# One quantising chain a step, base products copied straight into the residual's rows, and two reorderings in a GPS layer kernel

## The chip, the cores and the metric

The kernel runs on one core of a Trainium2 chip. The metric is the device time of one execution in microseconds, lower is better. TensorE is called PE here, VectorE DVE, ScalarE ACT, GpSimd POOL and SyncE SP. Before the change three runs took 913.72, 914.22 and 915.47 us, median 914.22 us.

## The reference

There are 1250 nodes with 1024 features and 40,000 directed edges sorted by target. Cut to what matters:

```python
xn  = layernorm(x)                                            # 1250 x 1024
# graph attention, 4 heads of 64, each node also an edge to itself
h   = (xn * rsqrt(mean(xn**2) + 1e-6) * rms_w) @ W_down       # 1250 x 256
e   = einsum(leaky_relu((h@Wl)[src] + (h@Wr)[dst]), att)
gnn = segment_sum(softmax_by_dst(e) * (h@Wl)[src], dst) @ W_up
# linear attention without softmax: 16 heads of 64
mix = (per head (q @ k.T) * 1/8 @ v) @ Wo.T + bo              # q, k, v = xn @ W.T + b
x2  = x + gnn + mix
# feed-forward part in fake fp4: blocks of 16 values, an fp8 scale for each
g, u   = nvfp4_linear(ln(x2), gate_w), nvfp4_linear(ln(x2), up_w)   # 1250 x 512
out    = x2 + nvfp4_linear(silu(g) * u, down_w)
```

`nvfp4_linear` takes the largest absolute value of each block of 16, makes an fp8 scale from it, divides, rounds to the fp4 values (0, 0.5, 1, 1.5, 2, 3, 4, 6 with sign), multiplies by the scale again, and multiplies the matrices.

## The kernel before, in words

The nodes lie in 10 chunks (0 to 9) of 128 rows, one row a partition. The program of each engine is written out by hand; semaphores alone tie the engines together, so each engine does its instructions in the order of the code.

**Start.** SP loads x chunk by chunk. DVE takes each chunk's mean and variance (L1271 to L1274), POOL the root (L573), and `norm(c)` (L1266) normalises it; in the code `norm(c-1)` stands behind chunk c's statistics. PE turns the normalised chunk (L772), ACT copies it to `xhat_t` (L1075), and the first product groups (L749) multiply it by W_down, which ACT has scaled (L1080). `one_hots(q)` (L1305) on DVE makes marks with which PE counts receivers (L757).

**Products and rounds.** Since the linear attention has no softmax, its matrices are folded together: 16 groups each of `gram`, `p`, `kv`, `t1`, `t2`, then 2 short `bias` groups and 14 `base` groups, which are x-hat times the folded matrix for chunks 0 to 6 (EARLY = 7), two halves of 512 columns each. A group is 8 fp32 products with 512 columns (16 records in the trace) into one PSUM bank; group n uses the bank of group n-4 and waits until DVE or ACT has taken that. ACT takes the base groups into the memory of `xhat_t`, DVE the bias groups. Beside this DVE, ACT and POOL run the graph attention in 62 rounds (number 61 is the last). A planner (`round_of`, from L982) walks over the groups with costs (PRODUCTS_AT, GROUP_STEP) and sets in which round each taking stands.

**Between.** When the rounds end, `send_attention` (L660) scatters the last chunk of the attention to HBM by an indirect DMA, SP loads the whole attention back (L523, tile `acc_sb`), and PE turns it (L918). Meanwhile the residual's rows `base` (part of tile `big_b`) are put together by DMA: SP writes the bias row into chunks 0 to 8 (L520), POOL adds x by 10 accumulating DMAs (`add_x`, L682) and then adds the base products by 7 more (`lay_base`, L688, 128x8x128 elements from `xhat_t`).

**Feed-forward steps.** `x2(c, h)` on PE (L908) makes a half chunk of the attention's product; for c >= 7 it first makes 8 fp32 products of the linear part (L905). `residual` on DVE (L1603) adds it to `base`. X2_PLAN says in which step each of them stands. Steps k = -1 to 12 then do, each engine in its own order:

- DVE: `tail_scales(k)` (hidden product L1569, block maxima L1258 on 512 and on 1024 columns, nine small operations L1223 to L1233 on up to 96 columns), `rows_rounded(k+1)` (eight operations L1247 to L1255 on 1024 columns, gives q), residuals of (k, 1), `hidden_rounded(k-1)` (the same eight on 512 columns, gives h), residuals of (k, 2).
- PE: turn q of chunk k+1 (L927), the x2 halves of (k, 0), turn h (L949) and multiply down (L960) for chunk k-2, gate and up products for chunk k+1 (L938).
- ACT: copy the turned q (L1164), normalise chunk k+2 (L1023, L1024), copy the turned h (L1191), silu of chunk k+1 (L1199), scale the down product (L1156); `deviation` (L1141 to L1146) takes the variance of a chunk as soon as its residuals are in.
- POOL: the root (L714) behind each deviation, and the DMA that adds the scaled product to the stored x2 (L720). The last chunk is finished on DVE (L1608).

## Time and profile before

| | before |
|---|---|
| median of three runs | 914.22 us (913.72 to 915.47) |
| the profiled execution's own time | 911.83 us |
| its span | 910.0 us |
| granted TensorE clock, mean | 0.972 of full speed |
| PE busy | 857.1 us (94%) |
| DVE busy | 818.1 us (90%) |
| ACT busy | 550.7 us (61%) |
| POOL busy | 500.0 us (55%) |
| bytes moved by DMA | 118.37 MB, mean 130 GB/s |

The span is the time from the first to the last recorded instruction; what lies around it is 911.83 - 910.0 = 1.83 us. Busy shares are means over stages with different limits: of the page's 40 slices of 22.75 us, PE shows 7 tenths in the 32nd (705 to 728 us), where DVE, in the slices 31 to 33, shows 6, 0 and 6; in the feed-forward slices behind it DVE shows 9 until the last, PE 5 to 9.

### The profile page before, as it was taken

The numbers are of one execution on the slowest core, as the hardware profiler recorded it, in microseconds if no ns is written. First come the engines' busy times: TensorE is split into PE (matmuls) and PEld (weight loads), VectorE is DVE, ScalarE is ACT, GpSimd is POOL, SyncE is SP. The second block draws the span as 40 slices with busy tenths as digits, with TensorE's granted clock in tenths as the row PEclk, the third lists the DMA queues.
The fourth block names the chain that finished last, engine by engine and source line by source line (L and its number), as shares of the span: only waits on it lengthen the run. The fifth ranks groups of instructions, "written<-read, shape, count | busy, mean of one in ns | idle before, by whom it ended". The sixth has DMA issues, their size and how long they took to land.

```text
span 910.0 us, 9566 instructions
## 1 busy us (share of the span) xinstructions
PE 857.1 (94%) x2744; PEld 419.5 (46%) x2754; DVE 818.1 (90%) x987; ACT 550.7 (61%) x1949; POOL 500.0 (55%) x529
## 2 busy tenths in 40 slices
PE   5999999999999999999999999998999797999755
PEld 5895455644444444444444444443444343444322
DVE  6999996789999999999999999999996069999996
ACT  3313123356677877779898988888998053343342
POOL 3400658577666767877777787877774400010011
PEclk7999999999999999999999999999999899999878
DMA  9322525463655433663336633339939970122224
GB/s 299 109 95 54 173 92 181 142 199 90 81 170 180 103 88 90 193 218 94 101 100 192 193 97 100 101 91 237 356 97 196 191 133 24 63 53 56 39 46 88
DMA packets 73443, 118.37 MB, mean 130 GB/s; under 512 B 29399, under 2 KB 43380, under 8 KB 73370
## 3 DMA queue, kind: packets, MB, share of 16 engines
q0 software_dynamic: 28560, 64.21, 30.5%
q1 hardware_dynamic: 44826, 53.52, 18.3%
q8 instruction: 22, 0.36, 0.2%
q14 instruction: 35, 0.29, 0.1%
HBM read 89.15 MB, written 17.17 MB: 117 GB/s over the span
## 4 chain that ended last, share of the span: by engine, by line
DVE 50%; PE 32%; POOL 7%; issue 6%; DMA 3%; ACT 1%; SPq 0%; ACTq 0%; DVEq 0%; POOLq 0%
PE acc L749 22%; DVE acc_sb L1498 9%; DVE z L1650 9%; DVE turned L1490 8%; DVE turned L1648 8%; POOL round_mem L551 6%; PE turned L905 2%; PE acc L908 1%; DVE round_mem L1258 1%; DVE round_mem L1247 1%; PE acc L938 1%; PE turned L960 1%; DVE big_a L1458 1%; DVE z L1655 1%; DVE round_mem L1248 1%
## 5 line engine op out<-in xcount | busy, mean ns | idle before, releaser
L551 POOL DMA_INDIRECT round_mem<-msg_table,idx x352 | 347.9, 988 | 99.8 <-issue 80.6
L1133 ACT ACTIVATE round_mem<-round_mem,pz 128x65 f32<-128x65 f32 x1408 | 353.9, 398 | 6.4 <-DVE acc_sb L1498 2.5
L749 PE MATMUL acc<-wslot,big_a 128*128 128x512 f32 x512 | 220.3, 592 | 0.0
L749 PEld LDWEIGHTS acc<-wslot,big_a 128*128 128x128 f32 x512 | 97.1, 190 | 121.5 <-issue 121.3
L1498 DVE TENSOR_REDUCE acc_sb<-round_mem 128x260 f32<-128x1820 f32 (+1 forms) x62 | 121.6, 1961 | 7.6 <-ACT round_mem L1133 5.1
L1123 ACT ACTIVATE pz<-z 128x7 f32<-128x7 f32 (+1 forms) x248 | 55.4, 296 | 93.7 <-DVE z L1655 93.4
L749 PE MATMUL acc<-wslot,big_b 128*128 128x512 f32 x256 | 110.0, 592 | 0.0
L749 PE MATMUL acc<-big_b,wslot 128*128 128x512 f32 x256 | 110.0, 592 | 0.0
L1490 DVE TENSOR_TENSOR turned<-round_mem,turned 128x1560 f32<-128x1560 f32 (+1 forms) x62 | 105.4, 1701 | 3.7 <-DMA round_mem<-msg_table,idx 1.6
L1650 DVE TENSOR_REDUCE z<-turned 128x24 f32<-128x1560 f32 (+1 forms) x62 | 105.1, 1695 | 2.1
L1648 DVE SCALAR_TENSOR_TENSOR turned<-turned,att_sb 128x1536 f32<-128x1536 f32 (+1 forms) x62 | 103.5, 1670 | 0.0
L749 PE MATMUL acc<-big_a,xhat_t 128*128 128x512 f32 x224 | 96.6, 593 | 2.7 <-ACT big_a L1070 2.7
L749 PE MATMUL acc<-big_b 128*128 128x512 f32 (+3 forms) x240 | 80.4, 494 | 0.0
L749 PEld LDWEIGHTS acc<-big_b,wslot 128*128 128x128 f32 x256 | 48.6, 190 | 61.2 <-issue 61.0
L749 PEld LDWEIGHTS acc<-wslot,big_b 128*128 128x128 f32 x256 | 48.6, 190 | 61.2 <-issue 61.2
L749 PEld LDWEIGHTS acc<-big_a,xhat_t 128*128 128x128 f32 x224 | 42.4, 190 | 56.9 <-issue 52.4
L714 POOL TENSOR_TENSOR rstd<-small,minus_half 128x1 f32<-128x1 f32 x10 | 6.4, 639 | 98.7 <-ACT small L1146 98.7
L749 PEld LDWEIGHTS acc<-big_b 128*128 128x128 f32 x240 | 42.8, 193 | 35.2 <-issue 29.5
L669 POOL TENSOR_TENSOR round_mem<-acc_sb,pz 128x260 f32<-128x260 f32 x62 | 45.9, 740 | 21.0 <-DVE acc_sb L1498 20.2
L720 POOL DMA_DIRECT2D out_x<-acc_sb x9 | 7.9, 878 | 71.2 <-ACT acc_sb L1156 71.2
L1060 ACT COPY big_a<-acc 128x512 f32<-128x512 f32 x16 | 9.2, 586 | 57.8 <-PE acc L749 42.3
L1199 ACT ACTIVATE round_mem<-acc,cscale 128x512 f32<-128x512 f32 x10 | 6.9, 688 | 59.3 <-PE acc L938 59.3
(233 smaller groups left out, 1031.6 us busy)
## 6 DMA issues: line engine op xcount, KB each, us to landing
round_mem<-msg_table,idx POOLq DMA_INDIRECT x352, 2.8
big_b<-in_x SPq DMA_DIRECT2D x9, 512.0 KB, 8.8
big_b<-big_b SPq DMA_DIRECT2D x9, 512.0 KB, 14.0
big_b<-in_x POOLq DMA_DIRECT2D x9, 512.0 KB, 12.4
out_x<-big_b SPq DMA_DIRECT2D x9, 512.0 KB, 3.6
out_x<-acc_sb POOLq DMA_DIRECT2D x9, 512.0 KB, 5.4
wslot<-in_wv_t SPq DMA_DIRECT2D x2, 2048.0 KB, 10.5
wslot<-in_wk_t SPq DMA_DIRECT2D x2, 2048.0 KB, 9.6
```

Of the source, the lines that this page charges most:

```text
L551: pool.indirect_dma_start(xg[g % 4][:, j, :], None, msg_table, bass.IndirectOffsetOnAxis(idx[:, c, j0 + j:j0 + j + 1], 0)).then_inc(xg_in[ ...
L669: nc.gpsimd.tensor_tensor(halves_of[g % 3][:, :, :, n].rearrange("p i (h d) -> p i h d", d=MR), running[c].rearrange("p (i h d) -> p i h d ...
L749: mm = nc.tensor.matmul(o(acc[:, n % 4, :]), a, b, start=first, stop=last)
L905: nc.tensor.matmul(to, xhat_t[:, k, c * NC:(c + 1) * NC], mat_a[:, k, h * HALF:(h + 1) * HALF], start=(k == 0), stop=False)
L908: mm = nc.tensor.matmul(to, gnn_tr[:, k, c * NC:(c + 1) * NC], wup_sb[:, k, h * HALF:(h + 1) * HALF], start=(c < EARLY and k == 0), stop=( ...
L1060: nc.scalar.copy(mat_a[:, m, h * HALF:(h + 1) * HALF], a).then_inc(t, 1)
L1123: ins = nc.scalar.activation(pz[:, g % 2, 0:slots + 1, h], z[:, g % 3, 0:slots + 1, h], ACT.Exp, scale=-1.0, bias=z[:, (g + 1) % 3, top_sl ...
L1133: ins = nc.scalar.activation(to[:, :, j], xg[g % 4][:, j, h * HR + 1:(h + 1) * HR], ACT.Copy, scale=pz[:, g % 2, j, h:h + 1])
L1490: return nc.vector.tensor_tensor(m4[:, 0:n], xg[g % 4][:, 0:n, :].rearrange("p j (h d) -> p j h d", d=HR)[:, :, :, 0:MR], receiver.unsquee ...
L1498: nc.vector.tensor_reduce(running[c].rearrange("p (i f) -> p i f", i=2), halves_of[g % 3][:, :, :, 0:n + 1], AX.X, ALU.add).then_inc(sum_d ...
L1648: step(nc.vector.scalar_tensor_tensor(m4[:, 0:slots, :, 1:MR], m4[:, 0:slots, :, 1:MR], 0.0, att_sb[0:NC].unsqueeze(1).to_broadcast([NC, s ...
L1650: step(nc.vector.tensor_reduce(zz[:, 0:slots, :], m4[:, 0:slots], AX.X, ALU.add))
```

## The change

It does five things.

1. **One chain a step.** The normalised rows and silu/hidden of a step now lie side by side in one slab of 1536 columns. The block maximum is one instruction, the first seven quantising operations run once on 1536 columns, and the eighth is split: q (1024), then h (512). `step_rounded` stands right behind `tail_scales`, ahead of the residual of (k, 1).
2. **Base products in place.** ACT copies the base groups straight into `base`. The bias row is no longer written first but added: SP loads x plainly for chunks 7 and 8 only, POOL adds x for chunks 0 to 6 and 9 (`add_x`) and the bias row for chunks 0 to 8 (`add_bias`). The 7 DMAs of `lay_base` are gone; of these 512 KB DMAs 19 are left of 26. Six stand ahead of the last scatter, three x behind the attention's load, ten in steps -1 and 1.
3. **Order of the base groups.** Both first halves of chunks 0 and 1 come ahead of the bias groups; the second halves, which need the last `t2` takings, behind them.
4. **Gated rows turned right behind q.** `turn_hidden(k-2)` stands right behind `turn_q(k+1)` ahead of the x2 products; ACT normalises chunk k+2 before it copies the turned q, and silu waits for h_done instead of hid_done.
5. **Start.** `norm(1)` stands ahead of chunk 2's statistics.

```diff
-PRODUCTS_AT, GROUP_STEP = 169, {"p0c": 2.0, "bias": 1.0}
+PRODUCTS_AT, GROUP_STEP = 166, {"p0c": 2.0, "bias": 1.0}
...
-BIAS_SUMS_AT, X_AT = 40, 61
+BIAS_SUMS_AT, AHEAD = 40, 3
+BETWEEN = {-2: {"x": (0, 1, 2), "bias": ()}, -1: {"x": (), "bias": (0, 1)}, 0: {"x": (), "bias": (2,)}}
...
-         "base": [(c, h) for c in range(EARLY) for h in range(2)]}
+         "base": [(c, h) for h in range(2) for c in range(2)] + [(c, h) for c in range(2, EARLY) for h in range(2)]}
...
-    g += [("bias", 0, "dve"), ("bias", 1, "dve")] + [("base", i, "act") for i in range(2 * EARLY)]
+    g += [("base", i, "act") for i in range(2)] + [("bias", i, "dve") for i in range(2)]
+    g += [("base", i, "act") for i in range(2, 2 * EARLY)]
...
+        NB = (D + I) // QB
+        slab = [tail_mem[0:NC, i * (D + I):(i + 1) * (D + I)] for i in range(2)]
+        ln2, silu = [a[:, 0:D] for a in slab], [a[:, D:D + I] for a in slab]
+        row_cells, row_steps = (tail_mem[0:NC, 6 * I + 768 * i:6 * I + 768 * (i + 1)].bitcast(BF16) for i in range(2))
...
-            sp.wait_ge(acc_taken["dve"], taken[index_of["bias", 1]])
-            for c in range(C - 1):
-                sp.dma_start(base[:, c, :], bias_bc).then_inc(x_in[c], 16)
+            sp.wait_ge(acc_full, index_of["bias", 1] + 1)
+            for c in range(EARLY, C - 1):
+                sp.dma_start(base[:, c, :], x[c * NC:(c + 1) * NC, :]).then_inc(x_in[c], 16)
...
             def add_x(c):
                 n = rows(c)
-                if c < C - 1:
-                    pool.wait_ge(x_in[c], 32)
+                if c < EARLY:
+                    pool.wait_ge(acc_taken["act"], taken[index_of["base", ORDER["base"].index((c, 1))]])
                 else:
                     for i in range(C - 1):
-                        pool.wait_ge(x_in[i], 32)
-                pool.dma_start(base[0:n, c, :], x[c * NC:c * NC + n, :], accum_op=ALU.add).then_inc(x_added[c], 16)
-
-            def lay_base(c):
-
-                pool.wait_ge(acc_taken["act"], taken[index_of["base", ORDER["base"].index((c, 1))]])
-                pool.wait_ge(x_added[c], 16)
-                pool.dma_start(base[:, c, :].rearrange("p (k n) -> p k n", k=KB), base_at[c], accum_op=ALU.add).then_inc(base_added[c], 16)
+                        pool.wait_ge(bias_added[i], 16)
+                pool.dma_start(base[0:n, c, :], x[c * NC:c * NC + n, :], accum_op=ALU.add).then_inc(x_added[min(c, EARLY)], 16)
+
+            def add_bias(c):
+
+                if c < EARLY:
+                    pool.wait_ge(x_added[c], 16)
+                else:
+                    pool.wait_ge(x_in[c], 32)
+                pool.wait_ge(acc_taken["dve"], taken[index_of["bias", 1]])
+                pool.dma_start(base[:, c, :], bias_bc, accum_op=ALU.add).then_inc(bias_added[c], 16)
...
-                if X_AT <= g < X_AT + C - 1:
-                    add_x(g - X_AT)
             for g in range(LAST - 2, LAST + 1):
+                for c in BETWEEN[g - LAST]["x"]:
+                    add_x(c)
+                for c in BETWEEN[g - LAST]["bias"]:
+                    add_bias(c)
                 rescale(g)
-                if g == LAST - 2:
-                    for c in range(max(LAST + 1 - X_AT, 0), C):
-                        add_x(c)
             for c in range(C):
                 if LAST_OF[c] + 5 > LAST:
                     send_attention(c)
-            for c in range(EARLY):
-                lay_base(c)
+            pool.wait_ge(gnn_in[1], 16)
+            for c in range(AHEAD, 6):
+                add_x(c)
...
             for k in range(-2, C + 2):
                 for c in whole_at((k, 0)):
                     deviation_root(c)
+                    if k == -1:
+                        add_bias(AHEAD + c)
+                if k == -1:
+                    for c in range(6, EARLY):
+                        add_x(c)
+                    for c in (5, *range(EARLY, C - 1), *range(6, EARLY)):
+                        add_bias(c)
+                if k == 1:
+                    add_x(C - 1)
...
             pe.wait_ge(bias_summed, KB)
-            for h in range(2):
-                group("bias", h, [(lambda a: a, minus_half[:, 0:1].to_broadcast([P, P]), bias_part[:, h * HALF:(h + 1) * HALF], True, True)])
-
             for i in range(2 * EARLY):
                 c, h = ORDER["base"][i]
-                if i in (0, 1):
+                if i == 2:
+                    for n in range(2):
+                        group("bias", n, [(lambda a: a, minus_half[:, 0:1].to_broadcast([P, P]), bias_part[:, n * HALF:(n + 1) * HALF], True, True)])
+                if i in (0, 2):
...
-            def down(c):
+            def turn_hidden(c):
...
+                if 1 <= k - 2 < C:
+                    turn_hidden(k - 2)
...
+                if k == 2:
+                    turn_hidden(0)
...
-                    act.wait_ge(acc_full, index_of["base", ORDER["base"].index((c, 1))] + 1)
-                    nc.scalar.copy(base_at[c][:, 4 * h:4 * h + 4, :], a.rearrange("p (k n) -> p k n", k=4)).then_inc(t, 1)
+                    nc.scalar.copy(base[:, c, h * HALF:(h + 1) * HALF], a).then_inc(t, 1)
...
+                if 2 <= k + 2 < C:
+                    normalize(k + 2)
                 if 0 <= k + 1 < C:
                     turn_over(k + 1)
-                if 2 <= k + 2 < C:
-                    normalize(k + 2)
...
-                        act.wait_ge(hid_done, c - 1)
+                        act.wait_ge(h_done, c - 1)
...
-                if c >= 1:
-                    norm(c - 1)
+                if c == 1:
+                    norm(0)
+                if c != 2 and c >= 1:
+                    norm(max(c - 1, 1))
...
-                    nc.vector.scalar_tensor_tensor(hidden, acc[0:NC, 3, :], cscale[0:NC, 1:2], silu[c % 2], ALU.mult, ALU.mult).then_inc(hid_done, 1)
+                    nc.vector.scalar_tensor_tensor(silu[c % 2], acc[0:NC, 3, :], cscale[0:NC, 1:2], silu[c % 2], ALU.mult, ALU.mult).then_inc(hid_done, 1)
                     dve.wait_ge(hid_done, c + 1)
-                    ins = block_max(tail_max[:, D // QB:], hidden)
                 if k + 1 < C:
                     dve.wait_ge(ln2_done, k + 2)
-                    ins = block_max(tail_max[:, 0:D // QB], ln2[(k + 1) % 2])
-                step(ins)
+                step(block_max(tail_max[:, lo:hi], slab[(k + 1) % 2][:, lo * QB:hi * QB]))
...
+            def step_rounded(k):
+                lo, hi = 0 if k + 1 < C else D // QB, NB if k - 1 >= 0 else D // QB
+                n = hi - lo
+                dve.wait_ge(tail_scaled, k + 2)
+                sc8, inv = (f[:, lo:hi] for f in tail_factors[k % 2])
+                v = slab[(k + 1) % 2][:, lo * QB:hi * QB]
+                by_block = v.rearrange("p (b i) -> p b i", i=QB)
+                high = v.bitcast(U16).rearrange("p (b i t) -> p i b t", i=QB, t=2)[:, :, :, 1]
+                cell, way = row_cells[:, 0:n * QB], row_steps[:, 0:n * QB]
+                step(nc.vector.tensor_tensor(by_block, by_block, inv.unsqueeze(2).to_broadcast([NC, n, QB]), ALU.mult))
+                step(nc.vector.tensor_scalar(cell.bitcast(U16).rearrange("p (i b) -> p i b", i=QB), high, CELL, MIDDLE, ALU.bitwise_and, ALU.bitwise_or))
+                step(nc.vector.tensor_scalar(way.bitcast(U16), cell.bitcast(U16), BINADE, HALF_BIT, ALU.bitwise_and, ALU.bitwise_or))
+                step(nc.vector.tensor_scalar(way, way, 1.5, 64.0, ALU.max, ALU.mult))
+                step(nc.vector.tensor_tensor(cell, cell, way, ALU.add))
+                step(nc.vector.tensor_tensor(way, cell, way, ALU.subtract))
+                step(nc.vector.tensor_scalar(way, way, -FP4_MAX, FP4_MAX, ALU.max, ALU.min))
+                way = way.rearrange("p (i b) -> p i b", i=QB)
+                for there, to, b0, b1, done in ((k + 1 < C, q_bf, 0, D // QB, q_done), (k - 1 >= 0, h_bf, D // QB, NB, h_done)):
+                    if there:
+                        if done is q_done and k >= 1:
+                            dve.wait_ge(q_tp, k)
+                        if done is h_done and k >= 3:
+                            dve.wait_ge(h_tp, k - 2)
+                        nc.vector.tensor_tensor(to[(k + 1) % 2].rearrange("p (i b) -> p i b", i=QB), way[:, :, b0 - lo:b1 - lo],
+                                                sc8[:, b0 - lo:b1 - lo].unsqueeze(1).to_broadcast([NC, QB, b1 - b0]), ALU.mult).then_inc(done, 1)
...
-                if 0 <= k + 1 < C:
-                    rows_rounded(k + 1)
+                if k <= C:
+                    step_rounded(k)
...
-                if 0 <= k - 1 < C:
-                    hidden_rounded(k - 1)
```

Three places where instructions move, as the engines' programs have them. First POOL around the end of the rounds; L669 is `rescale` of rounds 59 to 61 and L660 the last scatter. Before:

```order
L682 DMA big_b<-in_x 128x1024 [waits x_in7]
L682 DMA big_b<-in_x 128x1024 [waits x_in8]
L682 DMA big_b<-in_x 98x1024 [waits x_in5,x_in4,x_in6,x_in3,x_in7,x_in2,x_in8,x_in1,x_in0]
L669 TENSOR_TENSOR round_mem<-acc_sb,pz 128x260 [waits e_done,sum_done]
L669 TENSOR_TENSOR round_mem<-acc_sb,pz 128x2x130 [waits e_done,sum_done]
L660 DMA gnn_dram<-xr_sb,node_pi 1280x256 [waits gnn_norm]
L688 DMA big_b<-xhat_t 128x8x128 [waits x_added0,acc_taken_act]
L688 DMA big_b<-xhat_t 128x8x128 [waits x_added1,acc_taken_act]
```

In the changed program L668 is `rescale`, L659 the scatter, L681 `add_x` and L690 `add_bias`:

```order
L681 DMA big_b<-in_x 128x1024 [waits acc_taken_act] x3
L668 TENSOR_TENSOR round_mem<-acc_sb,pz 128x260 [waits e_done,sum_done]
L690 DMA big_b<-big_b 128x1024 [waits acc_taken_dve,x_added0]
L690 DMA big_b<-big_b 128x1024 [waits acc_taken_dve,x_added1]
L668 TENSOR_TENSOR round_mem<-acc_sb,pz 128x260 [waits e_done,sum_done]
L690 DMA big_b<-big_b 128x1024 [waits acc_taken_dve,x_added2]
L668 TENSOR_TENSOR round_mem<-acc_sb,pz 128x2x130 [waits e_done,sum_done]
L659 DMA gnn_dram<-xr_sb,node_pi 1280x256 [waits gnn_norm]
L681 DMA big_b<-in_x 128x1024 [waits acc_taken_act,gnn_in1]
L681 DMA big_b<-in_x 128x1024 [waits acc_taken_act] x2
```

Seven x additions stood closely ahead of the last scatter, and seven additions of products behind it; now three of x and three of the bias stand ahead, and the next waits for the attention's load (gnn_in1).

Second DVE in one feed-forward step. Before, from the last of the small operations:

```order
L1233 SCALAR_TENSOR_TENSOR round_mem<-round_mem 128x96 [waits dve_step]
L1247 TENSOR_TENSOR round_mem<-round_mem 128x1024 [waits q_tp,tail_scaled]
L1248 TENSOR_SCALAR round_mem<-round_mem 128x1024 [waits dve_step]
L1249 TENSOR_SCALAR round_mem<-round_mem 128x1024 [waits dve_step]
L1250 TENSOR_SCALAR round_mem<-round_mem 128x1024 [waits dve_step]
L1251 TENSOR_TENSOR round_mem<-round_mem 128x1024 [waits dve_step]
L1252 TENSOR_TENSOR round_mem<-round_mem 128x1024 [waits dve_step]
L1253 TENSOR_SCALAR round_mem<-round_mem 128x1024 [waits dve_step]
L1255 TENSOR_TENSOR round_mem<-round_mem 128x1024 [waits dve_step]
L1247 TENSOR_TENSOR round_mem<-round_mem 128x512 [waits tail_scaled]
L1248 TENSOR_SCALAR round_mem<-round_mem 128x512 [waits dve_step]
```

Of the changed kernel the same place:

```order
L1244 SCALAR_TENSOR_TENSOR round_mem<-round_mem 128x96 [waits dve_step]
L1602 TENSOR_TENSOR round_mem<-round_mem 128x1536 [waits tail_scaled]
L1603 TENSOR_SCALAR round_mem<-round_mem 128x1536 [waits dve_step]
L1604 TENSOR_SCALAR round_mem<-round_mem 128x1536 [waits dve_step]
L1605 TENSOR_SCALAR round_mem<-round_mem 128x1536 [waits dve_step]
L1606 TENSOR_TENSOR round_mem<-round_mem 128x1536 [waits dve_step]
L1607 TENSOR_TENSOR round_mem<-round_mem 128x1536 [waits dve_step]
L1608 TENSOR_SCALAR round_mem<-round_mem 128x1536 [waits dve_step]
L1616 TENSOR_TENSOR round_mem<-round_mem 128x1024 [waits q_tp,dve_step]
L1616 TENSOR_TENSOR round_mem<-round_mem 128x512 [waits h_tp]
```

Sixteen operations have become nine; q (the 1024 of L1616) now comes behind operations that carry h's columns too.

Third ACT around one silu. Before, L1199 is silu, L1141 to L1146 a deviation, L1164 the copy of the turned q, L1191 that of the turned h:

```order
L1199 ACTIVATE round_mem<-acc,cscale 128x512 [waits hid_done,gu_full]
L1156 ACTIVATE acc_sb<-turned,cscale 128x1024 [waits gt_tp,down_full]
L1141 ACTIVATE mean_var<-mean_var 128x1 [waits x2_taken]
L1142 ACTIVATE mean_var<-less_mean,mean_var 128x1 [waits act_step]
L1144 ACTIVATE round_mem,mean_var<-big_b,mean_var 128x1024 [waits act_step]
L1146 ACTIVATE small<-mean_var,eps_col 128x1 [waits act_step]
L1164 COPY round_mem<-turned 128x1024 [waits gu_full,q_tp]
L1023 ACTIVATE less_mean<-mean_var,rstd 128x1 [waits q_done,rstd2_done]
L1024 ACTIVATE round_mem<-big_b,less_mean,rstd 128x1024 [waits act_step]
L1191 COPY round_mem<-turned 128x512 [waits h_tp]
```

Of the changed kernel:

```order
L1210 ACTIVATE round_mem<-acc,cscale 128x512 [waits h_done,gu_full]
L1167 ACTIVATE acc_sb<-turned,cscale 128x1024 [waits gt_tp,down_full]
L1152 ACTIVATE mean_var<-mean_var 128x1 [waits x2_taken]
L1153 ACTIVATE mean_var<-less_mean,mean_var 128x1 [waits act_step]
L1155 ACTIVATE round_mem,mean_var<-big_b,mean_var 128x1024 [waits act_step]
L1157 ACTIVATE small<-mean_var,eps_col 128x1 [waits act_step]
L1035 ACTIVATE less_mean<-mean_var,rstd 128x1 [waits q_done,rstd2_done]
L1036 ACTIVATE round_mem<-big_b,less_mean,rstd 128x1024 [waits act_step]
L1175 COPY round_mem<-turned 128x1024 [waits gu_full,q_tp]
L1202 COPY round_mem<-turned 128x512 [waits h_tp]
```

The deviation stands behind silu in both; only the normalising has changed places with the copy of q.

## Rows read from the trace of the kernel before

**Rows 1.** Timeline, from 0 to 36 us: start us, us, engine, line, operation.

```profile
7.59 1.05 POOL L573 TENSOR_TENSOR rstd<-small,minus_half 128x1 f32<-128x1 f32 x1 [0.97 <-DVE small L1274]
...
8.98 1.07 ACT L1075 COPY xhat_t<-turned 128x512 f32<-128x512 f32 x2 [6.92 <-PE turned L772]
...
10.55 1.31 ACT L1080 ACTIVATE big_a<-big_a,rms_col 128x256 f32<-128x256 f32 x3 [0.49 <-DMA big_a<-in_w_down]
...
16.89 5.30 PE L749 MATMUL acc<-xhat_t,big_a 128*128 128x256 f32 x16 [0.68 <-ACT xhat_t L1075]
```

**Rows 2.** Timeline of DVE, then of PE, from 34 us.

```profile
56.63 1.48 DVE L1305 TENSOR_TENSOR big_a<-round_mem 125x2560 bf16<-125x2560 bf16 x1
...
60.13 2.15 PE L757 MATMUL turned<-big_a,xr_sb 125*40 125x32 bf16 x80
```

**Rows 3.** Timeline of PE, 560 to 704 us.

```profile
618.63 7.11 PE L749 MATMUL acc<-big_a,xhat_t 128*128 128x512 f32 x16 [2.01 <-ACT big_a L1070]
626.45 77.92 PE L749 MATMUL acc<-big_a,xhat_t 128*128 128x512 f32 x181 [0.72 <-ACT big_a L1070]
```

**Rows 4.** Timeline of PE and POOL, 672 to 745 us.

```profile
671.59 44.37 PE L749 MATMUL acc<-big_a,xhat_t 128*128 128x512 f32 x103
...
683.74 8.06 POOL L682 DMA_DIRECT2D big_b<-in_x  x9
```

**Rows 5.** The chain that ended last, 640 to 910 us: start us, us, what.

```profile
703.77 8.45 DMA gnn_dram<-xr_sb,node_pi
712.24 8.10 DMA acc_sb<-gnn_dram
...
721.63 3.75 PE turned L908 x4
725.38 2.43 PE acc L908 x4
...
728.25 1.72 PE acc L908 x4
```

**Rows 6.** Windows: busy PE, PEld, DVE, ACT, POOL; PE clock; DMA share; GB/s.

```profile
695.00:700.00 5.00, 5.00 (x13) 2.17 (x12) 0.45 (x1) 5.00 (x23) 0.66 (x1) 1.00 1.08 213
720.00:725.00 5.00, 4.49 (x8) 2.23 (x9) 0.00 (x0) 0.74 (x2) 0.00 (x0) 0.50 1.24 247
```

**Rows 7.** Issues of the attention's scatter and load.

```profile
DMA to landing us min/median/max: 2.4/3.1/14.1
```

**Rows 8.** Timeline of DVE in steps 0 and 1.

```profile
747.55 0.69 DVE L1603 SCALAR_TENSOR_TENSOR big_b<-turned,big_b 128x512 f32<-128x512 f32 x1 [4.17 <-PE turned L908]
...
760.79 0.75 DVE L1569 SCALAR_TENSOR_TENSOR round_mem<-acc,cscale,round_mem 128x512 f32<-128x512 f32 x1
...
766.36 1.22 DVE L1247 TENSOR_TENSOR round_mem<-round_mem 128x1024 f32<-128x1024 f32 x1
...
772.12 0.69 DVE L1247 TENSOR_TENSOR round_mem<-round_mem 128x512 f32<-128x512 f32 x1
...
775.72 0.68 DVE L1603 SCALAR_TENSOR_TENSOR big_b<-acc,big_b 128x512 f32<-128x512 f32 x1
```

**Rows 9.** Timeline of PE, ACT and DVE, 767 to 830 us.

```profile
772.26 1.04 PE L927 MATMUL turned<-identb,round_mem 128*128 128x128 bf16 x8 [5.24 <-DVE round_mem L1255]
...
773.08 9.47 PE L905 MATMUL turned<-big_a,xhat_t 128*128 128x512 f32 x16
...
789.48 0.69 ACT L1199 ACTIVATE round_mem<-acc,cscale 128x512 f32<-128x512 f32 x1 [13.67 <-PE acc L938]
...
793.34 1.24 ACT L1024 ACTIVATE round_mem<-big_b,less_mean,rstd 128x1024 f32<-128x1024 f32 x1
...
804.82 0.69 ACT L1199 ACTIVATE round_mem<-acc,cscale 128x512 f32<-128x512 f32 x1 [3.41 <-PE acc L938]
...
810.93 1.22 DVE L1258 TENSOR_REDUCE round_mem<-round_mem 128x64 f32<-128x1024 f32 x1 [0.83 <-ACT round_mem L1024]
```

**Rows 10.** Timeline of DVE, the eighth operation of q(9).

```profile
882.46 0.69 DVE L1255 TENSOR_TENSOR round_mem<-round_mem 128x1024 bf16<-128x1024 bf16 x1
```

40 lines of the change are left out of this document (8 added, 32 removed).

## The prediction

> **What bounds the kernel now.** I went through the profile from the end backwards. The page's busy shares (PE 94%, DVE 90%) name two limits and leave open where each holds, so I took the chain of waits for the places where the end is decided, and the timeline at each of them.
>
> The chain gives three stretches. Until the rounds end it runs over DVE; ahead of the feed-forward steps it is two DMAs, the last scatter of the attention (8.45 us) and its load (8.10 us), after which PE starts at 720.39 [rows 5]. PE is hardly earlier: its product groups end at 671.59 + 44.37 = 715.96 [rows 4], and it has worked without a gap since its first group at 16.89 [rows 1] but for two waits for `t2` takings, 2.01 and 0.72 us [rows 3]. So two paths end within 4.4 us of each other at 716 and 720, and the gain here is what the later of the two gains. From there to step k = 1 PE sets the pace: DVE waits 4.17 us for it at 747.55 [rows 8].
>
> I take the beginning of step k = 1 on DVE, 760.79 [rows 8], as a mark, S1. Behind it DVE is nearly full, but not alone: silu(2) waited 13.67 us for PE, and at 810.93 DVE waited 0.83 us for the normalised rows of ACT [rows 9]. The last q is done at 882.46 + 0.69 = 883.15 [rows 10]; from there to 910.0 the work is one chunk's latency, which the change leaves alone.
>
> **Start: -2.9 us for PE.** The first group waits for `xhat_t` of chunk 1. The root of chunk 1 was done at 7.59 + 1.05 = 8.64, so `norm(1)` need not wait for chunk 2's load, and its turning comes ahead of ACT's scaling of W_down, which ends at 10.55 + 1.31 = 11.86. ACT's copy of the turned chunk costs 1.07 (the row of chunk 0), so PE starts at 12.9 in place of 16.89, 3.9 earlier [rows 1]. Not all of it arrives: a count on PE at 60.13 needs marks that DVE makes until 56.63 + 1.48 = 58.11 [rows 2], and DVE gains only the 0.8 us of one normalising. 58.11 - 0.8 = 57.3 in place of 60.13 leaves 2.9.
>
> **Base order: -2.7 us for PE.** Two half groups and the bias groups now cover the `t2` takings; the waits were 2.01 + 0.72 [rows 3]. PE's base end becomes 715.96 - 2.9 - 2.7 = 710.4. The takings move to earlier rounds by the planner; on DVE the rounds' end gains 0.8 and loses about 1.1 to `p` takings that now find their bank not yet full (the groups come every 7.0 us), so the scatter is issued at 704.1 in place of 703.77. Bounds: -0.8 to +2.
>
> **Scatter and load: -9.8 us for the start of x2.** Before, nine additions of x were issued from 683.74 [rows 4], and at 695 to 700 us the DMA engines were fully busy at 213 GB/s [rows 6]; the scatter of 128 KB went behind them and took 8.45. At this rate 0.52 MB cost 2.5 us. The changed kernel puts six of them (15 us) ahead of rescale(59) to rescale(61), so they are through by about 699; the next three wait for the load. The scatter then costs what an undisturbed one costs, median 3.1 us of nine, between 2.4 and 14.1 [rows 7]; for the load of 256 KB I take the same 3.1 as an estimate, between 2.4 and 8.10 [rows 5, 7]. 704.1 + 6.2 = 710.3, the same as PE's 710.4. With the handing over I put the first turning at 710.6, which is 9.8 earlier. Here neither path hides the other's failure.
>
> By the Trainium skill ("DMA: Bandwidth & Descriptors", section "Anatomy of one DMA — SWDGE (gpsimd) path") a DMA costs 2.0 us and its bytes at 436 GB/s, which makes 2.3 and 2.6 us of the two. By that rule the load would land at 709.0, and PE's base end, 710.4, would decide: 0.2 us at most, since both ends meet there.
>
> **TensorE's clock: -2.6 us.** After the gap from 715.96 to 720.39 the window 720 to 725 shows the granted clock at 0.50, the lower level of 1.2 GHz [rows 6]; four products took 3.75 and the next four 2.43 where four later ones took 1.72 [rows 5]. That is 2.03 + 0.71 = 2.7 lost. The gap shrinks to well under 1 us, so I count 2.6 of it as regained; bounds 0 and 2.7. S1 comes at 760.79 - 12.4.
>
> The DMAs that stay behind it (three x, six bias, x for chunk 6 and 9) run beside the x2 products; each half's residual needs its chunk's. They are 19 in place of 26 and none has the 512-byte pieces of `lay_base`; I put them at nothing, with +2 as the upper bound.
>
> **The steps: +1.0 us.** Times here are from S1 = 0. The eight operations took 766.36 to 772.12 = 5.76 for 1024 columns, then 772.12 to 775.72 = 3.60 for 512 [rows 8]. Each is a fixed part and a part by the column: 512 columns more cost 2.16, so 1536 cost 7.92, and with the eighth split 8.0. Against 9.36 this saves 1.37, and the single block maximum 0.06: 1.43 a step, from 14.93 (760.79 to 775.72) to 13.50 without residuals of 0.61. Were DVE alone the bound, that would be 8 x 1.43 = 11.4.
>
> But q waits for h's columns now. It was done at 11.41 of a step (772.20), and will be at 13.24: 1.8 later. A second loop hangs on it: q, PE's turning, the x2 products, gate and up, silu, ACT's deviation of a later chunk, its root and its normalising, and DVE's next block maximum, which now needs hidden and rows together. Its terms [rows 9]: from PE's turning at 772.26 to silu(2) done at 790.17 it is 17.9; from silu(2) to silu(3) done (805.51) 15.34, in which PE is full; from silu(2) done to rows of chunk 4 ready 794.58 - 790.17 = 4.4, and 5.3 for chunk 5, by the wait that ended at 810.93, 5.4 behind it.
>
> - S2 = 15.3, S3 = 30.0 by DVE alone. silu(2) is done at 13.2 + 18.0 = 31.2, chunk 4's rows at 35.6, and DVE would want them at 30.8: wait 4.8, S3 counts as 34.85.
> - silu(3) 46.6, chunk 5's rows 51.9, wanted at 49.1: wait 2.8, S4 = 51.1. S5 = 65.9 by DVE.
> - silu(5) 79.9, chunk 7's rows 82.6: wait 1.8, S6 = 81.8; in the next step 1.3, S7 = 96.6. S8 = 110.2, and the last q is done at 123.4.
>
> Before, it was done at 883.15 - 760.79 = 122.4 [rows 8, 10]. So the 10.0 us that DVE saves until S8 are eaten by 10.7 us of such waits, and q's own delay of 1.8 makes the tail about 1.0 longer. The turning of h right behind q and the normalising ahead of the copy of q take 0.68 and about 0.9 out of this loop, which is in these figures; they don't shorten PE's 15 us.
>
> **Sum.** -9.8 - 2.6 + 1.0 = -11.4, against the profiled execution of 911.83 us (span 910.0): 900.4. The median of the runs is 2.4 above it: 914.22 - 11.4 = 902.8, and I say 902.7.
>
> **Rivals.**
>
> 1. *The steps stay bound by DVE.* If the deviations or PE come earlier in their steps than I have them, no wait of the second loop appears and the tail gives 112.6 for 122.4: -9.8. Sum -22.2, 892.0. For it: before, the rows of chunk 5 came only 0.83 us late [rows 9], so tenths on ACT decide there. Against it: in the first round of the loop silu waited 13.67 us for PE and PE 5.24 for q, so q's delay passes through.
> 2. *The DMA engines are not drained at the scatter.* The additions need base takings in rounds 55 and later; if they come late, six 512 KB additions lie ahead of the scatter as nine did. Scatter 8.45 and load 3.1 give 715.7, so -4.7 and no clock regained: -3.7, 910.5. If the load takes 8.10 too, x2 starts at 720.7 and the tail's +1.0 is left: 915.5, no change. For it: the largest landing of a scatter is 14.1 [rows 7]. Against it: 5 us of room by my count. The Trainium skill says of this on the same page ("Issuing engines are not separate DMA queues") that DMAs run on the same 16 engines and interleave whoever issues them; the 8.45 beside 3.1 agrees.
> 3. *Slower: PE falls to the lower clock in each step.* The turning of q comes 1.8 later, so PE idles longer ahead of it, and at 772.26 its wait of 5.24 was followed by 9.47 us for 16 records that took 7.11 elsewhere [rows 3, 9]. In the four steps with products behind the turning (k = 2 to 5) this would cost 4 x 2.4, and the same ratio on the gate and up products of about 4 us 4 x 1.36: +15.0 on the forecast, 917.7. It decides from a wait of some 3 us ahead of the turning in each of them. Against it: it was the first step with products behind the turning, and one step on PE was full from silu to silu, with 3.41 us of waiting on ACT's side in place of 13.67 [rows 9].
> 4. *The merged chain costs more than its columns say.* The split eighth operation reads rows with a stride over 96 blocks; if that costs 0.5 us a step, 8 x 0.5 = +4.0, 906.7.
>
> **How the numbers follow.** A difference under 0.2% (1.8 us, the spread of the three runs) can't be told from none. Chances: the forecast 0.48 (its own range 898 to 907); rival 1 0.20; rival 2 half-way 0.13 and in full 0.05; rival 3 0.07; rival 4 0.07. Faster: 0.48 + 0.20 + 0.13 + 0.07 = 0.88; same 0.05; slower 0.07. The range from 891 to 910 leaves out the full rival 2, rival 3 and part of the half-way one.
>
> **What would show it.** Right: PE's first product group near 13; no wait at its first base groups; the last scatter landing in about 3 us, PE's first turning of the attention near 710.6 with no stretch at clock 0.50 behind it; DVE's block maximum on 1536 columns waiting for ACT at k = 3, 4, 6 and 7, together 10 us; q done 13.2 us into a step. Wrong: steps of 13.5 us without such waits (rival 1), a scatter over 6 us (2), the sixteen L905 records at 9 us in more than one step (3), an eighth operation over 1.2 us for both parts (4).

## The result, and the profile after

The changed kernel took 908.12 us in the median of seven runs (904.46 to 909.87), the kernel before 913.38 (909.52 to 915.47): ratio 0.9947, 95% interval 0.9933 to 0.9961. It is faster by 4.8 us, where 11.4 were forecast. In a second set of runs (e9) it took 906.24 us, ratio 0.9925 (0.9908 to 0.9942); the mean of the two ratios, 0.9936, is 5.9 us. Below, microseconds against before are such ratios times 913.4, and the changed kernel stands with its mean, 0.9936, unless a set is named.

The first trace is of its fastest run: 904.46 us, span 902.3. It bears out the front of the forecast nearly word for word. The timeline there (start, duration, engine, line, operation, in brackets the idle time before and what ended it):

```profile
12.85 5.78 PE L760 MATMUL acc<-xhat_t,big_a 128*128 128x256 f32 x16 [1.40 <-ACT xhat_t L1086]
...
66.81 17.43 PE L760 MATMUL acc<-big_a 128*128 128x512 f32 x40
...
710.90 0.60 PE L929 MATMUL turned<-ident,acc_sb 128*128 128x128 f32 x4
712.10 1.96 PE L919 MATMUL turned<-wslot,xr_sb 128*128 128x512 f32 x4 [0.61 <-ACT xr_sb L1041]
```

PE's first group starts at 12.85 for 16.89 [rows 1], its first turning of the attention at 710.90 for 720.39. Its last product group ends at 711.06, so PE and not the attention's load is now the later path, by less than 1 us. The chain of waits and the window behind the turning, to be read beside [rows 5, 6]:

```profile
705.02 2.50 DMA gnn_dram<-xr_sb,node_pi
...
707.96 5.55 DMA acc_sb<-gnn_dram
```

```profile
720.00:725.00 5.00, 5.00 (x16) 2.42 (x15) 4.46 (x15) 4.68 (x10) 2.22 (x4) 1.00 1.07 238
```

The scatter takes 2.50 for 8.45; its 5.55 us of load are the larger part of 1 MB, the first landed before the turning. PE's clock is 1.00 where it was 0.50, and four x2 products take 1.96 in place of 3.75. What the forecast had put at nothing shows here, in POOL's timeline and DVE's:

```profile
725.89 3.29 POOL L690 DMA_DIRECT2D big_b<-big_b  x3 [0.46 <-DMA big_b<-in_x]
735.94 0.86 POOL L690 DMA_DIRECT2D big_b<-big_b  x1 [6.76 <-DMA big_b<-in_x]
```

```profile
738.17 0.69 DVE L1628 SCALAR_TENSOR_TENSOR big_b<-acc,big_b 128x512 f32<-128x512 f32 x1 [1.95 <-DMA big_b<-big_b]
...
750.80 0.75 DVE L1582 SCALAR_TENSOR_TENSOR round_mem<-acc,cscale,round_mem 128x512 f32<-128x512 f32 x1
```

Nine additions of 512 KB and two stores share the DMA engines from 713.8; the bias of chunk 5, wanted at 736, was issued at 725.89 and landed at 738.15, and the residual of step 0 waited 1.95 us for it. So S1, the beginning of step 1, is 750.80: 10.0 earlier, not 12.4. (Of the ten 512 KB DMAs that "The change" puts in steps -1 and 1, eight stand there; the other two are SP's plain loads of x, issued at 634.93.)

The traces of the experiments below show the price more cleanly. From the first turning to S1 it takes 39.6 to 40.0 us in the seven traces in which step 0 waits for such a DMA (this one, e2, e3, e5, e6, e9, e10), and 37.84 to 37.87 in nine in which it does not (e4, e7, e8, e11 to e16): 2 us. Before, it took 40.40, of which 2.7 were lost to the lower clock.

Then the steps, the merged chain first:

```profile
756.31 1.76 DVE L1602 TENSOR_TENSOR round_mem<-round_mem 128x1536 f32<-128x1536 f32 x1
...
763.35 1.03 DVE L1616 TENSOR_TENSOR round_mem<-round_mem 128x1024 bf16<-128x1024 bf16 x2
...
785.51 1.75 DVE L1269 TENSOR_REDUCE round_mem<-round_mem 128x96 f32<-128x1536 f32 x1 [3.58 <-ACT round_mem L1036]
```

```profile
764.10 1.03 PE L938 MATMUL turned<-identb,round_mem 128*128 128x128 bf16 x8 [7.08 <-DVE round_mem L1616]
764.93 8.61 PE L916 MATMUL turned<-big_a,xhat_t 128*128 128x512 f32 x16
```

From 756.31 to the last h the chain takes 8.0 us as forecast, and q is done 13.2 into the step. PE now waits 7.08 for q where it waited 5.24 [rows 9]. The products behind that wait take 8.61 us, less than the 9.47 of before. What got longer is the third group of such products after S1; the turning ahead of it waited 2.27 us (after, then before; the granted clock over the two is 0.81 and 1.00):

```profile
798.72 8.78 PE L916 MATMUL acc<-big_a,xhat_t 128*128 128x512 f32 x16
```

```profile
805.64 7.09 PE L905 MATMUL acc<-big_a,xhat_t 128*128 128x512 f32 x16
```

DVE waits 3.58 for ACT's rows at 785.51. The groups of DVE's lines from S1 to the last q (busy, mean ns, idle before and its releaser) give all of these waits, after and before:

```profile
L1602 DVE TENSOR_TENSOR round_mem<-round_mem 128x1536 f32<-128x1536 f32 x8 | 14.1, 1758 | 0.3
L1269 DVE TENSOR_REDUCE round_mem<-round_mem 128x96 f32<-128x1536 f32 x8 | 14.0, 1753 | 11.4 <-ACT round_mem L1036 11.3
```

```profile
L1247 DVE TENSOR_TENSOR round_mem<-round_mem 128x1024 f32<-128x1024 f32 (+1 forms) x16 | 15.3, 955 | 0.3
L1258 DVE TENSOR_REDUCE round_mem<-round_mem 128x32 f32<-128x512 f32 (+1 forms) x16 | 14.6, 948 | 1.1 <-ACT round_mem L1024 0.8
```

Six steps wait, 3.58, 2.88, 1.11, 0.90, 1.72 and 1.13 us, 11.3 together, against 0.8 before. The last q is done at 875.56, 124.8 us behind S1, where the forecast said 123.4 and before had 122.4; from there to the finish on DVE (897.01; before 904.64) it is 21.5 us, as before. That last figure is not fixed, as the section on the hardware shows.

### The profile page after: what moved, and what is told of

The parts are those of the page before. It is cut to its first block, busy times and chain, and to the rows that moved or that the text cites. A ratio compares the mean times of both kernels' runs of the same rounds, so it can differ in the third digit from the quotient of the medians.

```text
span 902.3 us, 9485 instructions
## 1 busy us (share of the span) xinstructions
PE 854.7 (95%) x2744; PEld 419.3 (46%) x2754; DVE 810.3 (90%) x923; ACT 550.5 (61%) x1949; POOL 496.6 (55%) x529
## 4 chain that ended last, share of the span: by engine, by line
DVE 47%; PE 37%; issue 5%; POOL 4%; DMA 3%; ACT 3%; SPq 0%; ACTq 0%; DVEq 0%; POOLq 0%
PE acc L760 29%; DVE acc_sb L1511 8%; DVE z L1673 8%; DVE turned L1503 7%; DVE turned L1671 7%; POOL round_mem L550 3%; PE acc L949 2%; PE turned L973 2%; PE acc L916 2%; DVE round_mem L1269 1%; DMA big_b<-big_b 1%; DVE big_a L1471 1%; ACT round_mem L1144 1%; DMA big_b<-in_x 1%; DVE big_b L1660 1%
## 5 line engine op out<-in xcount | busy, mean ns | idle before, releaser
L668 POOL TENSOR_TENSOR round_mem<-acc_sb,pz 128x260 f32<-128x260 f32 x62 | 44.7, 721 | 20.3 <-DVE acc_sb L1511 19.5
L716 POOL TENSOR_TENSOR rstd<-small,minus_half 128x1 f32<-128x1 f32 x10 | 8.4, 842 | 67.1 <-ACT small L1157 67.1
```

Of the source, the lines that this page charges most:

```text
L668: nc.gpsimd.tensor_tensor(halves_of[g % 3][:, :, :, n].rearrange("p i (h d) -> p i h d", d=MR), running[c].rearrange("p (i h d) -> p i h d ...
```

## The experiments

Each kernel ran beside the one before on the same chip, in four sets; ratios are against it. Labels of one set: e1 to e4, e5 to e8, e9 to e12, e13 to e16.

**One part at a time: e1 and e2.** e1 is before with the merged steps, e2 the changed kernel with the steps of before:

```diff
 e2:
-                if k <= C:
-                    step_rounded(k)
+                if 0 <= k + 1 < C:
+                    rows_rounded(k + 1)
                 for i in added_at((k, 1)):
                     residual(*i)
+                if 0 <= k - 1 < C:
+                    hidden_rounded(k - 1)
```

> The kernel before with parts 1 and 4 of the change alone (slab, one chain a step, turning of h right behind q, order of ACT's normalising); start, base products and DMAs as before. Theory L (a second loop over PE and ACT eats DVE's saving; in the changed kernel DVE waited 3.58, 2.88, 1.11, 0.90, 1.72 and 1.13 us for ACT's normalised rows): the same as before or slower by 1 to 3 us, and the same waits of DVE in the trace. Rival D (the steps are bound by DVE and the gain of the change lies there): 8 to 10 us faster than before.

> The changed kernel with parts 1 and 4 undone: start, base order, base copies and DMAs changed, the steps' two chains and orders as before. Theory L: step k = 1 begins about 10 us earlier than before and the tail behind it is as long as before (122.4 us to the last q), so 9 to 11 us faster than before and 2 to 5 us faster than the changed kernel. Rival D: under 3 us faster than before, since the merged chain is what gains.

Measured: e1 914.96 us, ratio 1.0021 (1.0005 to 1.0037), 1.9 us slower. e2 903.50 us, ratio 0.9892 (0.9877 to 0.9908), 9.9 us faster than before and 4 us faster than the changed kernel. All of the gain is the front's; the merged steps cost 1.9 alone and 4.0 on the new front. Rival D is out. e1's first two waits on DVE for the rows are those of the changed kernel; the later ones are 1.78, 0.61 and 2.07, with 1.24 for silu:

```profile
794.84 1.75 DVE L1262 TENSOR_REDUCE round_mem<-round_mem 128x96 f32<-128x1536 f32 x1 [3.56 <-ACT round_mem L1028]
...
811.21 1.75 DVE L1262 TENSOR_REDUCE round_mem<-round_mem 128x96 f32<-128x1536 f32 x1 [2.89 <-ACT round_mem L1028]
```

**Which loop, e3, e5, e6.** e3 moves ACT's deviations of (k, 1) and (k, 2) ahead of silu. e5 and e6 leave five groups of products out, on the changed kernel and on e2:

```diff
 e5, e6:
-                if c >= EARLY:
+                if c >= EARLY and (c, h) == (7, 1):
                     for k in range(KB):
                         nc.tensor.matmul(to, xhat_t[...], mat_a[...], ...)
```

> The changed kernel with ACT's deviations of (k, 1) and (k, 2) ahead of the silu of the same step in place of behind it. Theory L: deviation and root of chunks 4, 5, 7 leave the loop from silu to the normalised rows, some 2.7 us in each of two steps and 1 in others; DVE's waits of 3.58 and 2.88 fall to about 1; 4 to 6 us faster than the changed kernel, 9 to 11 faster than before. Rival P (PE sets the pace of the steps, the waits of DVE for ACT only mirror it): within 1.5 us of the changed kernel. Rival C (PE's lower clock grows with every wait): gain above 6.

> The changed kernel without the 8 fp32 products of the linear part for five of the six half chunks of chunks 7 to 9, those made in steps 1 to 5; they are left out of the result. Theory P (in the steps PE is full: 15.3 us from silu to silu, so DVE's waits of 11.5 us only mirror PE, and moving ACT's deviation moved the waits but not their sum): PE has 7 us to spare in each step, steps take 13.5 us and 0.6 for each residual, the waits vanish; the tail from step 1 to the last q falls from 124.7 to about 113 us; 10 to 13 us faster than the changed kernel. Theory L alone (latency over ACT's deviation and normalising): the 3.6 and 2.9 us waits stay, since PE's share of the loop shrinks but the deviation still stands behind silu; at most 7 us faster.

> The kernel with the two chains and the old orders in the steps and the changed front (e2), with the same products left out of the result as in e5. Theory P: its steps are bound by DVE and stay at 14.9 us and residuals, so it is within 2 us of e2, and the merged chain of e5 is 8 to 10 us better than this. Rival: PE bounds the old steps too and this gains 5 us or more on e2.

Measured: e3 907.73 us, 0.9929 (0.9915 to 0.9944), 0.6 us better than the changed kernel: the expectation of theory L failed, and the time is rival P's. Its waits moved and their sum stayed (11.4 us). One of them shows a link that I had not seen, POOL's root behind POOL's addition to the stored rows, which itself waits for ACT's scaling behind silu:

```profile
801.14 0.94 POOL L722 DMA_DIRECT2D out_x<-acc_sb  x1 [4.52 <-ACT acc_sb L1167]
801.79 0.88 POOL L716 TENSOR_TENSOR rstd<-small,minus_half 128x1 f32<-128x1 f32 x1
```

```profile
804.38 1.75 DVE L1269 TENSOR_REDUCE round_mem<-round_mem 128x96 f32<-128x1536 f32 x1 [3.75 <-ACT round_mem L1036]
```

e5 took 897.37 us, 0.9836 (0.9813 to 0.9859), 9 us better than the changed kernel, more than theory L allowed and a little less than theory P said; e6 903.71, 0.9897 (0.9874 to 0.9920), as e2. In e5 the hidden product, with which DVE begins a step, starts 14.1, 14.1 and 13.5 us after the last one:

```profile
811.49 0.75 DVE L1582 SCALAR_TENSOR_TENSOR round_mem<-acc,cscale,round_mem 128x512 f32<-128x512 f32 x1
...
825.61 0.74 DVE L1582 SCALAR_TENSOR_TENSOR round_mem<-acc,cscale,round_mem 128x512 f32<-128x512 f32 x1
...
839.71 0.75 DVE L1582 SCALAR_TENSOR_TENSOR round_mem<-acc,cscale,round_mem 128x512 f32<-128x512 f32 x1
...
853.22 0.74 DVE L1582 SCALAR_TENSOR_TENSOR round_mem<-acc,cscale,round_mem 128x512 f32<-128x512 f32 x1
```

Two waits of 1.1 us are left in its eight steps, and from S1 to the last q it is 115.5 us, 9.3 less than in the changed kernel; theory P had said 113. So PE's products are part of what bounds the changed steps 1 to 5, and they do not bound the old ones. They are not all of it: e14, below, keeps the products and still comes to step 5 on DVE 2.2 us sooner behind S1 than e13. Without its products the merged chain is worth 5.6 us (e5 against e6; 8 to 10 were expected), with them it is worth less than nothing.

**The additions' order: e4, e11, e13.** e4 leaves the late bias additions out; e11 (on e2) and e13 (on the changed kernel) put them in the order in which the residuals want them:

```diff
 e11, e13:
-            for c in range(AHEAD, 6):
+            for c in (5, 3, 4):
                 add_x(c)
...
-                        add_bias(AHEAD + c)
+                        add_bias((5, 3)[c])
                 if k == -1:
-                    for c in range(6, EARLY):
-                        add_x(c)
-                    for c in (5, *range(EARLY, C - 1), *range(6, EARLY)):
+                    for c in (7, 4):
+                        add_bias(c)
+                    add_x(6)
+                    for c in (6, 8):
                         add_bias(c)
```

> The changed kernel without the six additions of the bias row for chunks 3 to 8: for these chunks the bias is left out of the result. Theory L says that step 0's residual waited for them (landing 12.3 us after issue, at 738.15), so step k = 1 begins 2 to 2.6 us earlier and the kernel is 2 to 3 us faster than the changed one. Rival: the time is given back in the loop of the steps, within 1 us of the changed kernel.

> The front alone (e2) with POOL's additions behind the attention's load in the order in which the residuals want them: x 5, 3, 4, bias 5, 3, 7, 4, x 6, bias 6, 8, in place of x 3, 4, 5, bias 3, 4, x 6, bias 5, 7, 8, 6. Theory: the 2.1 us that step 0's residual waited for bias 5 vanish and step 1 begins 2 us earlier, 1.5 to 2.5 us faster than e2. Rival: PE or the engines of the DMA set it anyway, within 0.7 us of e2.

> The changed kernel with POOL's late additions in the order of e11. Theory: the 1.8 to 2.0 us wait of step 0's residual vanishes, 1 to 2.6 us faster than the changed kernel (e4, without the late bias additions, was 2.4 faster, e11 1.3 faster than e2); 904 to 906 us where before is 913.4. Rival: given back in the steps, no difference.

Measured: e4 905.86 us, 0.9919 (0.9898 to 0.9941); e11 902.14, 0.9881 (0.9864 to 0.9899); e13 903.76, 0.9910 (0.9884 to 0.9936). Against their bases that is 1.6, 1.0 and 2.4 us, each within the intervals' width, so the times of e4 and e11 fall between theory and rival and only e13's is the expected one. The traces decide: in all three step 0's wait for a DMA is gone, and the way from the first turning to S1 is 37.8 us for 39.9 and 40.0. The cost forecast as nothing is 2 us there, 1 to 2.4 by the times, and the order alone gives it back.

**The planner's beginning and the start: e7, e8, e9, e10.** e7 sets PRODUCTS_AT back to 169; e8 does so and undoes part 5; e10 undoes part 5 alone; e9 is the changed kernel again.

```diff
 e8, e10:
-                if c == 1:
-                    norm(0)
-                if c != 2 and c >= 1:
-                    norm(max(c - 1, 1))
+                if c >= 1:
+                    norm(c - 1)
```

> The changed kernel with the planner's beginning (PRODUCTS_AT) at 169 as before in place of 166: the second taking of p leaves round 0, where DVE waited 1.5 to 2.9 us for PE. Theory: the start of the x2 products hangs on PE's last base group (711.06 and the first turning at 710.90), so this is within 1 us of the changed kernel though the rounds end 1 to 3 us earlier. Rival: the rounds' end sets it, 1.5 to 3 us faster.

> The changed kernel with part 5 undone (norm(1) behind chunk 2's statistics) and the planner's beginning at 169. The forecast counted 2.9 us for this part; in the traces so far PE's lead at 171 us was 2.7, 0.8, 1.3 and -0.3 us, since the clock granted around 80 to 100 us was lower where PE was earlier. Theory: 0.5 to 2 us slower than the changed kernel. Rival: 2.5 to 3 us slower, the whole lead.

> The changed kernel itself once more. In six other kernels with its start, PE's p groups began at 172.2 to 174.9 us, in its own first trace at 170.8. Theory: the first trace was an early one; here they begin at 172 to 174, the x2 products 540.2 us behind that (712 to 714), and step 1 at 752 to 754 in place of 750.8, with the same steps behind it. Rival: 170.8 and 750.8 again, and the runs' scatter comes from the tail.

> The changed kernel with part 5 alone undone (norm(1) behind chunk 2's statistics), the planner's beginning left at 166. Theory (of PE's lead of 2 to 2.9 us at 67 us, 1.65 is given back to the lower clock before 115 us): 0.5 to 1.5 us slower than the changed kernel. Rival (the forecast's term): 2.5 to 3 us slower.

Measured: e7 910.90 us, 0.9973 (0.9960 to 0.9987); e8 912.69, 1.0000 (0.9986 to 1.0013); e10 909.84, 0.9953 (0.9937 to 0.9970). e7 came out against both its theory and its rival: it is 3.4 us slower than the changed kernel. Its planner puts the takings of the first base groups a round later (the first at 633.45 for 627.39), and PE waits for their banks:

```profile
634.17 8.80 PE L760 MATMUL acc<-big_a,xhat_t 128*128 128x512 f32 x16 [2.95 <-ACT big_b L1078]
```

x2 then begins at 718.79, 544.4 us behind the first p group. The three units in the table are a part of the change as large as any other. e8, which has the old table and the old start, is 5.8 us slower than the changed kernel, beyond its theory and its rival. Two comparisons within a set give part 5 alone 2.6 us (e10 against e9) and 2.5 us (e8 against e7), about the 2.9 of the forecast; against the mean of the changed kernel's two sets e10 gives 1.6. The times speak against my later theory, 0.5 to 1.5 us. The traces settle it less: PE's first gram group starts at 67.4 us in the mean of the fourteen with the new start and at 70.0 in the four with the old one, its first p group at 172.3 and 174.0, so the lead is 2.5 us there and 1.7 later. e9's own trace has PE's p groups at 173.70 in place of 170.81, S1 at 753.49 and the same waits behind it, so the first trace was an early one, as expected:

```profile
753.49 0.74 DVE L1582 SCALAR_TENSOR_TENSOR round_mem<-acc,cscale,round_mem 128x512 f32<-128x512 f32 x1
...
788.56 1.75 DVE L1269 TENSOR_REDUCE round_mem<-round_mem 128x96 f32<-128x1536 f32 x1 [3.58 <-ACT round_mem L1036]
...
804.91 1.75 DVE L1269 TENSOR_REDUCE round_mem<-round_mem 128x96 f32<-128x1536 f32 x1 [2.89 <-ACT round_mem L1036]
...
900.46 1.28 DVE L1633 SCALAR_TENSOR_TENSOR big_b<-turned,cscale,big_b 128x1024 f32<-128x1024 f32 x1 [4.32 <-PE turned L973]
```

**Merging late steps only: e12.** As e11, with the merged chain from step 6 on.

> As e11, but in steps 6 to 10, where no x2 product is left on PE, the seven operations run once on 1536 columns; steps up to 5 keep two chains; PE and ACT in the order of before, hidden in silu's place, so that silu waits for h. Theory P (the merged chain pays where PE is not full): steps 6 to 8 at 13.5 in place of 14.9, less 1.8 for the last q: 1.5 to 3 us faster than e11. Rival L: ACT's normalised rows come late and the steps stay at 14.9: the same as e11 or up to 2 us slower.

Measured: 907.12 us, 0.9933 (0.9917 to 0.9950), 4.7 us slower than e11. With ACT in its old order DVE waits 1.46 us for it in step 4, which is not merged yet (0.67 in e11), and 1.69, 2.71 and 3.01 in the merged ones. Up to the last q the trace is 3.7 us longer than e11's. The direction is rival L's, the size beyond it. So in the steps without x2 products on PE another link binds, which e14 looks for.

**The rows early, the last q alone: e14, e15, e16.**

```diff
 e14, e15, ACT:
-                if 2 <= k + 2 < C:
-                    normalize(k + 2)
...
                 for c in whole_at((k, 0)) if k >= 0 else []:
                     deviation(c)
+                for c in [*whole_at((k, 1)), *whole_at((k, 2))] if k >= 0 else []:
+                    deviation(c)
+                if 2 <= k + 3 < C:
+                    normalize(k + 3)
...  silu(k+1), scale_down(k-2)
 e14, e15, POOL:
+                for c in [*whole_at((k, 1)), *whole_at((k, 2))]:
+                    deviation_root(c)
                 if 0 <= k - 2 < C - 1:
                     add_to_stored(k - 2)
 e15, e16, DVE:
+                if k == 8:
+                    rows_rounded(k + 1)
+                    hidden_rounded(k - 1)
-                if k <= C:
+                elif k <= C:
                     step_rounded(k)
```

> e13 with ACT's deviations of (k, 1) and (k, 2) and the normalising of chunk k+3 ahead of the silu of step k, and POOL's roots ahead of its addition to the stored rows. Theory: DVE never waits for the rows again; up to step 5 it waits for silu instead, since PE is full there (15.3 us), and from step 6 on the steps fall from 15 to 13.5 or 14.1: 3 to 5 us faster than e13. Rival P2 (PE's chain of turning, gate and up, silu is the bound in the late steps too): within 1 us of e13.

> e14 with two chains in step 8 alone, the last q first and then h. Theory: the last q is done 1.8 us earlier and the last chunk's latency hangs on it: 1 to 2 us faster than e14. Rival: h of chunk 7 then comes later by 0.4 and the end hangs on it or on the order of PE, no difference.

> e13 with two chains in step 8 alone, the last q first and then h. Theory as for e15: 1 to 2 us faster than e13. Rival: no difference.

Measured: e14 899.93 us, 0.9849 (0.9827 to 0.9870), 5.6 us better than e13; from S1 to the last q its trace takes 118.3 us for e13's 124.3, and its steps 7 and 8 take 13.5. Which of its moves does it (ACT's deviations, its normalising, POOL's roots) no run separates; e3 shows that the deviations alone do not. e16 901.72, 0.9884 (0.9860 to 0.9907), 2.4 better than e13. e15 895.11, 0.9796 (0.9771 to 0.9822), 4.8 better than e14: nearly all of the last step's wait for silu is gone in it; that it gives more here than in e16 lies within the intervals. The traces up to the last q say 2.0 us for it and 1.8 for e16, as expected. e15 is the best version run, 18.6 us (2.0%) faster than before. The waits on DVE in its steps are two of silu, where PE is full, and one small one:

```profile
780.33 0.75 DVE L1583 SCALAR_TENSOR_TENSOR round_mem<-acc,cscale,round_mem 128x512 f32<-128x512 f32 x1 [1.17 <-ACT round_mem L1213]
...
796.54 0.75 DVE L1583 SCALAR_TENSOR_TENSOR round_mem<-acc,cscale,round_mem 128x512 f32<-128x512 f32 x1 [2.62 <-ACT round_mem L1213]
...
840.32 0.75 DVE L1583 SCALAR_TENSOR_TENSOR round_mem<-acc,cscale,round_mem 128x512 f32<-128x512 f32 x1 [0.54 <-ACT round_mem L1213]
...
853.84 0.74 DVE L1583 SCALAR_TENSOR_TENSOR round_mem<-acc,cscale,round_mem 128x512 f32<-128x512 f32 x1
...
868.73 0.75 DVE L1583 SCALAR_TENSOR_TENSOR round_mem<-acc,cscale,round_mem 128x512 f32<-128x512 f32 x1
...
875.99 0.75 DVE L1583 SCALAR_TENSOR_TENSOR round_mem<-acc,cscale,round_mem 128x512 f32<-128x512 f32 x1
...
888.11 1.28 DVE L1648 SCALAR_TENSOR_TENSOR big_b<-turned,cscale,big_b 128x1024 f32<-128x1024 f32 x1 [4.78 <-PE turned L974]
```

From 840.32 to 853.84 a step is 13.5 us. From 868.73 to 875.99 it is 7.3, as in the kernel before; e14, with its last q late, has a wait of 3.25 there and 10.6. The early rows with two chains in every step were not run; in e11's trace DVE waits only 0.67 us for the rows, so little is left there for them to gain.

## Why the forecast was wrong

- **Scatter, load, clock: right.** First turning 710.90 for 710.6, scatter 2.50 for 3.1, clock 1.00. By the Trainium skill ("DMA: Bandwidth & Descriptors", section "Anatomy of one DMA — SWDGE (gpsimd) path") the scatter would take 2.3 us; with 2.50 the trace is nearer to that than to my 3.1. PE's base end decides, as it would by that rule. The Trainium skill gives this sum in that section for the path of POOL's DMAs; the load, for which the forecast also used it, is issued by SP, and its 256 KB took 2.8 us.
- **Base order: right, with 2.2 us for 2.7.** From its first p group to its last product group PE takes 540.2 us for 542.5; one wait of 0.71 us is left ahead of the second bias group. It hangs on the planner's three units, which the forecast passed over as "earlier rounds by the planner" (e7).
- **Start: right in size,** 2.6 us (e10 against e9) and 2.5 (e8 against e7) for 2.9; 60.13 less 57.3 is in truth 2.8. But the rounds' end did not stay at 704.1: the scatter was issued at 705.02, in e9 at 707.87 and in e10 at 710.78, since the second taking of p in round 0 waits for PE (DVE waits 1.49, 2.59 and 5.93 us there). It costs nothing, because PE comes as late.
- **"I put them at nothing, with +2 as the upper bound": wrong.** It is the upper bound that came. Step 0 waits 1.95 us for the bias, the way from the first turning to S1 shortens by 2 us in every trace without that wait, and the times of e4, e11 and e13 put it at 1.0 to 2.4 us. The forecast had the rate, 2.5 us an addition, and did not set the nine of them, some 22 us, against the 22 us until the residual wants the bias.
- **"The steps: +1.0": wrong in size, and the step that failed most.** The mechanism stood as it was forecast (3.58 and 2.88 for 4.8 and 2.8, q at 13.2, 11.3 us of waits for 10.7), but the sum came out at +2.4 in the first trace, +3.1 in e9's (146.97 us from S1 to the finish for 143.85), and 4.0 by the runs (e2 against the changed kernel). Set beside the forecast's table, the first trace is still 0.7 us ahead at S6 (81.1 for 81.8) and falls behind only then: S7 96.9 for 96.6, S8 111.5 for 110.2, the last q 124.8 for 123.4. Of this turn 0.6 is a residual in step 6 that the table leaves out, and 0.4 and 1.13 are waits at S7 (1.72 for 1.3) and at S8, where the forecast had DVE as the bound and no wait. What held DVE there was ACT's normalising behind silu, in step 8 with the deviation and root of its chunk; in e14, where all of them are early, steps 7 and 8 take 13.5 us.
- **PE's lower clock is rival 3 in small, but not the cause of the missing 1.4 us.** The sixteen products took 8.61 and 8.78 us in two steps and 7.1 in the others. Before, it was 9.47 in one step and 7.1 in the others, so PE lost 0.8 us more on these products in all, and in steps in which the trace is ahead of the table.
- **What of it is not settled:** between 2.4 and 3.1 us of the traces and 4.0 of the runs I can name no single cause. The intervals of the runs overlap, and the way from the last q to the finish alone differs by 2.1 us between traces of the same instructions, as the last section shows. Of the missing 5 to 6 us about 3 are the steps, 1 to 2.4 the additions, and the rest lies within the scatter of the start below.

Rival 1 (DVE-bound steps, 892.0) is out by e1, rival 2 by the scatter of 2.50, rival 4 by the 1.03 us of both parts of the eighth operation.

## What to carry to other kernels

Work saved on an engine that looks full is worth only what the loop behind it lets through: before merging two chains, ask which result of the first was waited for, and how much later it comes now. Count the waits of a step by leaving a suspected engine's work out in both versions (e5, e6). And when the bound has moved, the order of small things on the other engines (a root behind a store, a normalising behind silu, additions in the order of their number) is worth more than the large edit: here, with the last q taken out of the merged chain, 12.8 us against 5.9.
